# ScalarE's fill of the score buffer moved to just ahead of the first exponentials in the three steady blocks of a Mamba, attention and expert kernel

## The reference

```python
x = x + mamba(layernorm(x))            # in_proj, convolution, selective scan with 16 states, gate, out_proj
x = x + cross_attention(layernorm(x), ctx, ctx, position_ids, mask)   # 32 heads of 128, 8 key/value heads, rotary
x = x + experts(layernorm(x))          # 64 experts of rank 8, top 16

# inside the Mamba layer
ssm_p = xc @ x_proj_w.T                # 32 columns for dt, 16 for B, 16 for C, each RMS-normed
dt = softplus(dt_r @ dt_proj_w.T + dt_bias)
h = exp(dt * A) * h + dt * B * x       # over 64 tokens, 1024 channels, 16 states
y = (sum over states of h * C + D * xc) * silu(z)

# inside the attention
scores = where(mask == 0, -1e9, q @ k.T / sqrt(128))
probs = softmax(scores)
```

## Time and profile before

| what | value |
|---|---|
| median of 3 runs | 2321.03 us (2320.09 to 2322.94) |
| the profiled execution's own time | 2319.86 us |
| its span in the profile | 2318.3 us |
| busy: PE, DVE, ACT, POOL | 90%, 76%, 44%, 30% of the span |
| granted TensorE clock over the span | 0.951 of full speed |

### The profile page before, as it was taken

One profiled execution on the slowest core, in us unless ns is written; L12 is line 12 of the kernel. 1 busy time (PEld: TensorE's weight loads), 2 busy tenths in 40 slices (PEclk: granted clock), 3 DMA queues, 4 the chain that ended last, 5 costly groups with the idle time before them and its releaser, 6 DMA issues.

```text
span 2318.3 us, 26885 instructions
## 1 busy us (share of the span) xinstructions
PE 2083.2 (90%) x8268; PEld 1192.0 (51%) x8272; DVE 1767.5 (76%) x1783; ACT 1009.7 (44%) x2581; POOL 704.9 (30%) x492
## 2 busy tenths in 40 slices
PE   6877897898999989898999989998999989899998
PEld 2333454345556544345555544444655654478874
DVE  4499994459999996249999996429999996456653
ACT  2544441255555542155455550255555551144441
POOL 0289992501111111501111111600111110457750
PEclk9788999989999999989999999989999999899999
DMA  2579896427888874535888874635888885322220
GB/s 64 157 182 227 212 226 175 137 110 159 179 190 193 180 169 124 172 110 123 193 179 183 195 164 118 182 94 132 181 190 190 185 181 141 123 71 88 94 85 19
DMA packets 117810, 352.12 MB, mean 152 GB/s; under 512 B 14016, under 2 KB 14144, under 8 KB 115296
## 3 DMA queue, kind: packets, MB, share of 16 engines
q0 software_dynamic: 40704, 146.82, 32.7%
q1 hardware_dynamic: 70112, 191.68, 26.6%
q10 hardware_dynamic: 6912, 12.59, 1.4%
HBM read 197.68 MB, written 23.33 MB: 95 GB/s over the span
## 4 chain that ended last, share of the span: by engine, by line
DVE 33%; PE 31%; DMA 15%; issue 14%; ACT 3%; POOL 2%; DVEq 1%; PEldq 1%; SPq 0%; POOLq 0%; ACTq 0%; PEld 0%
DMA xc<-hs 12%; DVE hs L1262 11%; DVE hs L1474 5%; PE pq L1719 4%; DVE hs L1269 3%; PE acc L1674 3%; DVE hs L1253 3%; PE acc L1796 2%; PE pq L1727 2%; PE acc L1809 2%; PE pq L1964 2%; PE acc L1880 2%; PE pq L1757 2%; PE pk L1964 2%; DVE qr L1295 1%
## 5 line engine op out<-in xcount | busy, mean ns | idle before, releaser
L769 POOL DMA_DIRECT2D xc<-hs x192 | 164.1, 860 | 1110.5 <-DVE hs L1269 1090.4
L1262 DVE TENSOR_TENSOR_SCAN hs<-dA,hs 128x1024 f32<-128x1024 f32 x192 | 428.6, 2273 | 0.0
L994 ACT ACTIVATE dA<-dt,aneg 128x504 f32<-128x504 f32 x384 | 253.6, 707 | 312.3 <-DVE hs L1262 312.2
L1727 PE MATMUL pq<-qT,wa 128*128 128x512 f32 x768 | 354.9, 616 | 15.6 <-DVE pzsc L1337 14.9
L1809 PE MATMUL acc<-wb,oT 128*128 128x512 f32 x768 | 353.5, 605 | 3.6 <-ACT oT L982 3.6
L1269 DVE TENSOR_TENSOR hs<-hs,bc 128x1024 f32<-128x1024 f32 x256 | 307.4, 1202 | 2.2
L1727 PEld LDWEIGHTS pq<-qT,wa 128*128 128x128 f32 x768 | 146.8, 196 | 190.1 <-issue 178.1
L1674 PE MATMUL acc<-xnT,wa 128*128 128x512 f32 x512 | 232.6, 608 | 11.9 <-PE acc L1674 3.5
L1253 DVE TENSOR_TENSOR hs<-u,bc 128x1024 f32<-128x1024 f32 x192 | 227.2, 1216 | 20.6 <-DMA xc<-hs 15.0
L959 ACT ACTIVATE pr<-pzsc,mx 128x64 f32<-128x64 f32 x512 | 170.6, 336 | 120.6 <-DVE mx L1343 120.6
L1809 PEld LDWEIGHTS acc<-wb,oT 128*128 128x128 f32 x768 | 141.7, 194 | 148.7 <-issue 144.6
(11 more groups left out here) (255 smaller groups left out, 3336.8 us busy)
## 6 DMA issues: line engine op xcount, KB each, us to landing
xc<-hs POOLq DMA_DIRECT2D x240, 512.0 KB, 6.8
bc<-bc_rows SPq DMA_DIRECT2D x64, 512.0 KB, 7.5
wa<-in_wq SPq DMA_DIRECT2D x64, 512.0 KB, 9.9
wb<-in_wo SPq DMA_DIRECT2D x64, 512.0 KB, 6.3
wa<-in_wx SPq DMA_DIRECT2D x16, 512.0 KB, 6.5
wa<-in_wz SPq DMA_DIRECT2D x16, 512.0 KB, 3.7
wb<-in_ow SPq DMA_DIRECT2D x16, 512.0 KB, 6.7
wv<-in_wv SPq DMA_DIRECT2D x26, 256.0 KB, 12.8
```

The costliest lines, as they stand in the source:

```text
L769: G.dma_start(xc[:, 2 * c:2 * c + 2, :], hs[:, c, :].rearrange("p (d t) -> p d t", t=T), accum_op=ALU.add).then_inc(s_y[c], 16)
L994: ins = S.activation(to[:, :, 1:SEQ], dt[:, s, :].rearrange("p (b t) -> p b t", t=SEQ)[:, :, 1:SEQ], ACT.Exp, scale=aneg[:, s, bass.ds(jj ...
L1262: V.tensor_tensor_scan(out=hs[:, c, :], data0=dA[:, c % 2, :], data1=hs[:, c, :], initial=0.0, op0=ALU.mult, op1=ALU.add).then_inc(scd.sem, 1)
L1727: ins = M.matmul(pq[:, h, :], wa4(p)[:, k, h * P:(h + 1) * P], qT[:, k, :], start=(k == 0), stop=(k == KE - 1))
```

## The change

The fill of a steady stage is called just ahead of `exps(0, 0)`, behind the sixteen activations of the dt projection, instead of at the top of the stage. Stage 4 keeps its fill at the top. VectorE gets two waits ahead of its first queries, for the stores of the turned keys (`s_kst[0]` and `s_kst[1]`), since its products write `qp` and `qr`, which the even rounds' stores read.

```diff
--- before.py
+++ after.py
@@ -1021,7 +1021,7 @@
                     if mamba and attn and not tail and p == 1:
                         evac_v(jj + 1)
 
-                if attn:
+                if attn and not mamba:
                     prefill()
                 if mamba:
                     eng.wait_ge(ssd.sem, ssd.upto(i, 0))
@@ -1045,6 +1045,8 @@
                         S.activation(dt[:, s, :], acc[:, s % 4, :], ACT.Relu,
                                      bias=chan[:, 1, s:s + 1]).then_inc(dtv.sem, 1)
                 if attn:
+                    if mamba:
+                        prefill()
                     exps(0, 0)
                     if not mamba:
                         swap_q(0, 1)
@@ -1381,6 +1383,9 @@
                 if mamba:
                     ch = Chain(eng, ch_f, i)
                     ssm_rows(i)
+                if mamba and attn:
+                    for n in range(2):
+                        eng.wait_ge(s_kst[n], blk * 32 + 32)
                 if attn:
                     eng.wait_ge(s_mask, blk * 32 + 32)
                     eng.wait_ge(s_cs, blk * 32 + 32)
```

## The result

| | before | after |
|---|---|---|
| median of the runs | 2321.03 us (5 runs, 2320.09 to 2323.56) | 2311.56 us (5 runs, 2307.65 to 2314.16) |
| ratio to before, 95% interval | | 0.9961 (0.9946 to 0.9976) |
| the profiled execution's own time, its span | 2319.86, 2318.3 | 2314.16, 2312.6 |

The change makes the kernel faster by 9.5 us by the medians, 5.6 to 12.5 us by the interval.

The account below looks back on a forecast made before the run. The chain ending last was shared by VectorE, TensorE, DMA and issue time; stage 1's fill wait was the change's place. Gains 5.27 + 1.48 = 6.75 us from 2321.03 gave 2314.3 us, range 2311.8 to 2317.3.

Parts of the forecast that it names:

- the first term: Top of stage 1: squares no longer wait behind the fill, so the group mean starts 5.27 us earlier.
- The second term: Stage 1, group mean to first scans: without PE's standstill the clock is better, gaining 1.48 us, bounds 0 and 2.98.
- The rival that the head is long because it is a loop's first pass: Stage 1, group mean to first scans stays 75.23 us; gain only 4.3 to 5.3, time near 2315.8; chance 0.14.
- The rival that the clock gain is kept: Stage 1's dt projection still takes 8.94 us; gain 8.25, time 2312.8; chance 0.12 including a full-speed case.
- The sum: Whole kernel: 5.27 + 1.48 = 6.75 us gained, all of it in stage 1, giving 2314.3 us.
- What was put at nothing: Fill's new place, VectorE's two waits, the key loads' lateness, and stages 2 and 3: zero cost or gain.
- The fill at its new place: Ahead of the exponentials in three stages: costs zero, with 5.3 us to spare before VectorE's masking.
- The two waits and the key loads: Before stage 1's first queries and scores: zero cost, stores landing 7.8 us ahead, key loads with 13 us of room.
- The single points in time of the forecast: Expected starts: first scans of stage 1 at 518.5, group mean of stage 2 about 977.6, of stage 3 about 1509.9.
- A sign of being wrong that came up: Forecast wrong if stage 1's top gains 5 us but stage 2's group mean is less than 4.6 us early.
- The margin for the transfers: From stage 1's first scans on: shifting against the stream of transfers may add or take away 1.0 us.

Follow-up runs that it names:

- written-out kernels: Stages 1 and 2 written out instead of looped: on the changed kernel 2298.00 us, again 2302.57 us; on the kernel before, fill at the top, 2330.91 us.
- the late store: Two extra GpSimd passes ahead of stage 1's last turned-keys store: on the changed kernel 2319.04 us, on the kernel before 2329.98 us, one run each.
- keeping PE busy: Kernel before with six extra 128x512 products on PE behind the x_proj product in stages 1 and 2: 2317.53 us, one run.
- the fill's behind the root: Against the changed kernel, fill placed behind the square root and ahead of the value copy, not behind the dt activations: 2311.16 us, ratio 0.9972.
- the seven fills: Changed kernel with seven fills in a row instead of one at the new place in each steady stage: 2311.73 us, ratio 0.9959.

## Why the prediction was right, and where it was off

**The place and the first term.** The squares stood behind the fill, and had to wait there in stage 1 alone. This is shown: the move in stage 3 alone brings nothing that can be told; the squares and the root let past the fill bring what the whole change brings; a later store delays the group mean with the fill at the top, and not with the fill moved. Its size is where the sum was off. I took 5.27 us from the one trace at hand, a difference between the ends of two chains, one of which runs over DMA. In that trace GpSimd waited 2.45 us for the last raw keys, and the store landed 11.9 us behind the x_proj product's start. Eleven other executions without the delay, of both kinds of kernel, have 12.0 to 15.7, mean 13.8. It was the earliest of twelve. The three profiles that leave stage 1 as it was have the group mean 13.10, 16.34 and 15.42 us behind the product's start, 14.95 on average, and with the move it is 7.85: a term of **7.1 us**, of 5.3 to 8.5 from one execution to another. Three draws are few, and two things make 7.1 an upper estimate. The written-out kernels have late landings, 14.4 to 15.7; the nine executions with the loop and without the delay have 13.1 on average, which with the 1.2 us from landing to group mean makes a term of 6.4. And in the execution of stage 3 alone the x_proj product took 9.41 us, which was hidden, since the store landed later still; with the fill moved such a product shows in full, as in the late store's 83.72. By the standstills alone (6.02, 9.27 and 6.01, less 0.77) the three give 6.3. That the first profiles of before and after agreed with the sum to 0.15 us, 6.90 for 6.75, is luck: the landing in the one was the earliest of twelve.

**The second term.** 1.48 us forecast; heads of 75.23, 75.10, 75.29 and 75.22 with the standstill and 73.58, 73.57, 73.59, 73.58 and 73.58 with the fill moved and covered, loop kept: **1.63 us**. Right in size, and shown to be the clock by keeping PE busy. The rival that the head is long because it is a loop's first pass is answered a second time by the written-out kernel with the fill at the top, whose head is 75.10 with no loop. As stage 3 had it, the dt projection gives a part of the clock gain of 2.99 us back: it takes 10.6 to 11.1 us in stage 1 in every kernel with the fill moved, for 8.9. The rival that the clock gain is kept did not happen in stage 1 with the change. It happened elsewhere: 72.25 for the head of stage 1 with PE kept busy, 70.18 in stage 2 of the change run again.

**The sum.** 7.1 + 1.63 = 8.7 us, or 8.1 with the first term at 6.4. By the distances themselves: start to scans is 90.16 on average for those three profiles and 81.43 for the change's, its repeat's, the fill's behind the root and the seven fills'. The medians of these four kernels differ from those of the kernel before by 9.3 to 10.0 us, and their ratios give 9.1, 6.5, 6.5 and 9.5, each with an interval of some 3 to 4 us either way.

**What was put at nothing.** The fill at its new place costs nothing, and has 5.4 us of cover where 5.3 were worked out. The two waits and the key loads cost nothing that shows. The single points in time of the forecast held within about a microsecond up to the first scans (517.68 for 518.5), and not behind them: the group mean of stage 2 was due at 977.6 and came at 980.24, 4.1 us early instead of 6.75.

**A sign of being wrong that came up.** Less than 4.6 us at this point, with the 5 us at the top of stage 1 there, was to mean that the forecast is wrong. By this one pair of profiles it would be. But the sign compares two executions, and that point scatters by more than the term: over three profiles with stage 1 as it was (984.37, 991.18 and 986.46) and four with the gain (980.24, 981.94, 975.95 and 980.80) the means lie 7.6 us apart. The head start does reach the end; the sign was set too fine for one execution.

**The margin for the transfers.** 1.0 us, taken from two stretches of one execution, was too small. From first scans to the next x_proj product stage 1 takes 449.6 to 455.3 us in the eleven profiles with the loop, and whether the 1.1 us between the means of the two kinds is more than chance can't be told from so few. That spread, and that of the store's landing, should have widened the range; it ended a quarter of a microsecond short.

## What to carry to other kernels

Look down an in-order engine's list for a wait on something late and ask what cheap work behind it others are standing for: here the squares, an activation of 0.6 us, held TensorE for 6 to 9 us. The cure is to let them pass; how far back the waiting instruction goes is free until its own reader's cover (5.4 us here) is used up. And when a term of the sum is the difference between two engines' arrival times, one of them set by DMA, one trace gives one draw of it: bound it by how the same wait varies in other stages or rounds, not by a like-for-like stretch alone.

## What the runs showed of the hardware

- The granted clock of a short stretch differs between executions of one program. The dt projection (16 records of 512 columns) took 8.4 to 11.5 us in stages 2 and 3 of these profiles, at granted clocks from 0.83 (8.4 us) to 0.61 (11.5 us), and the x_proj product of stage 1 took 7.08 us in eleven of the fourteen profiles and 9.4 us, at a granted clock of 0.75, in three.
- A product that keeps PE busy can lose the clock while it runs: the dt projection of stage 1 started at a granted clock of 1.00 and was at 0.50 some 4 us later, with PE busy for all of it.
- The kernel before, timed 35 times in one comparison, spread from 2310.3 to 2328.6 us, far more than the 3.5 us of its first five runs. Five runs on each side gave the ratio an interval of 0.30% from end to end, and 12 against 35 gave 0.27%.
- A loop's branch back showed as 2.1 to 4.7 us of idle TensorE without a releaser, in stage 2 only, and was 0.84 us when the loop was written out. With the fill moved, the written-out kernel gained 9 to 14 us, so 5 us or more beyond this; with the fill at the top it was slower than the loop.
- Two kernels that differ in nothing of their last stage took 313 and 336 us from its fill to the end of the span, at mean granted clocks of about 0.96 and 0.91.
